# A chunked delta-rule recurrence on one core: states and deltas in two halves, another order of the calls, waits against constants

## What is computed

```python
def _step(Sm, inputs):
    q_t, k_t, v_t, beta_t = inputs
    Sk = jnp.einsum('bhde,bhe->bhd', Sm, k_t)
    delta = v_t - Sk
    Sm = Sm + beta_t[..., None] * jnp.einsum('bhd,bhe->bhde', delta, k_t)
    o_t = jnp.einsum('bhde,bhe->bhd', Sm, q_t)
    return (Sm, o_t)
_, outputs = jax.lax.scan(_step, S0, (q, k, v, beta))
return outputs @ wo + bo
```

## Time and profile before

| what | value |
|---|---|
| time, median of 3 runs (lowest to highest) | 3310.53 us (3310.06 to 3311.02) |
| profiled execution, first to last instruction | 3309.8 us |
| PE busy, weight loads busy | 3179.2 us (96%), 2594.1 us (78%) |
| DVE, ACT, POOL busy | 1841.6 us (56%), 1308.4 us (40%), 1205.1 us (36%) |
| recurrence, first and last small matmul of the stage | 962.7 and 1721.4 us |
| in it, first matmul of product 0 and of product 63 | 998.2 and 1717.9 us |

### The profile page before, as it was taken

One profiled execution on the slowest core, in us unless ns is written; L12 is line 12 of the kernel. 1 busy time (PEld: TensorE's weight loads), 2 busy tenths in 40 slices (PEclk: granted clock), 3 DMA queues, 4 the chain that ended last, 5 costly groups with the idle time before them and its releaser, 6 DMA issues.

```text
span 3309.8 us, 150288 instructions
## 1 busy us (share of the span) xinstructions
PE 3179.2 (96%) x68438; PEld 2594.1 (78%) x68438; DVE 1841.6 (56%) x2965; ACT 1308.4 (40%) x2654; POOL 1205.1 (36%) x1211
## 2 busy tenths in 40 slices
PE   5999999999958999999999999999999999999998
PEld 4777777777747888898888778887777888777886
DVE  6787878778648899888323333233333323333324
ACT  5444445444313333333343333333333433333333
POOL 1435564655526776666211222211222212122211
PEclk8999999999969999999999999999999999999999
DMA  3445555455465677666661110101110110111010
GB/s 111 144 148 167 141 162 154 145 152 162 139 201 181 220 227 228 215 197 207 200 184 35 39 39 13 39 26 39 39 39 17 36 39 26 39 39 38 14 39 26
DMA packets 388865, 356.00 MB, mean 108 GB/s; under 512 B 58256, under 2 KB 321680, under 8 KB 385680
## 3 DMA queue, kind: packets, MB, share of 16 engines
q1 hardware_dynamic: 386400, 351.86, 34.2%
q10 hardware_dynamic: 2224, 0.90, 0.2%
HBM read 184.65 MB, written 153.09 MB: 102 GB/s over the span
## 4 chain that ended last, share of the span: by engine, by line
PE 65%; DMA 2%; SPq 0%; DVE 0%; issue 0%; ACT 0%; DVEq 0%; ACTq 0%
PE bank L237 14%; PE bank L235 14%; PE bank L236 14%; PE bank L1238 13%; PE bank L1283 5%; PE bank L1698 2%; PE bank L1689 2%; DMA ringB<-heads_scratch 1%; PE bank L1681 1%; PE bank L1672 1%; DMA Z<-z_scratch 0%; DVE g L2010 0%; PE bank L1745 0%; SPq L1147 0%; ACT relu L1867 0%
## 5 line engine op out<-in xcount | busy, mean ns | idle before, releaser
L1939 DVE TENSOR_TENSOR glo<-gl,gh 128x512 fp32r<-128x512 f32 x256 | 196.0, 766 | 823.5 <-ACT gh L1817 821.8
L1813 ACT ACTIVATE gl<-bank,b1m 128x512 f32<-128x512 f32 x256 | 176.0, 687 | 736.4 <-PE bank L237 730.9
L235 PE MATMUL bank<-h,w_hi 128*128 128x512 f32 x1024 | 421.1, 411 | 0.1
L235 PE MATMUL bank<-w_hi,gh 128*128 128x512 f32 x1024 | 402.7, 393 | 0.9 <-DVE glo L1939 0.9
L237 PE MATMUL bank<-h,w_lo 128*128 128x512 f32 x1024 | 401.3, 392 | 0.0
L237 PE MATMUL bank<-w_hi,glo 128*128 128x512 f32 x1024 | 400.5, 391 | 0.0
L236 PE MATMUL bank<-h,w_hi 128*128 128x512 f32 x1024 | 399.4, 390 | 0.0
L236 PE MATMUL bank<-w_lo,gh 128*128 128x512 f32 x1024 | 399.2, 390 | 0.0
L236 PEld LDWEIGHTS bank<-h,w_hi 128*128 128x128 f32 x1024 | 193.4, 189 | 49.2 <-issue 10.7
L235 PEld LDWEIGHTS bank<-h,w_hi 128*128 128x128 f32 x1024 | 192.5, 188 | 48.7 <-issue 10.8
L1238 PE MATMUL bank<-ringA 32*32 32x32 f32 x16512 | 221.9, 196 | 5.3 <-issue 4.3
(11 more groups left out here) (200 smaller groups left out, 7086.1 us busy)
## 6 DMA issues: line engine op xcount, KB each, us to landing
ringB<-heads_scratch SPq DMA_DIRECT2D x257, 192.0 KB, 3.3
ringA<-heads_scratch SPq DMA_DIRECT2D x260, 128.0 KB, 2.8
X<-in_L_attn_x SPq DMA_DIRECT2D x16, 1024.0 KB, 10.1
x_scratch<-X SPq DMA_DIRECT2D x16, 1024.0 KB, 4.5
heads_scratch<-vb SPq DMA_DIRECT2D x16, 1024.0 KB, 5.2
heads_scratch<-qk SPq DMA_DIRECT2D x16, 1024.0 KB, 6.6
heads_scratch<-kb SPq DMA_DIRECT2D x16, 1024.0 KB, 5.2
heads_scratch<-kbuf SPq DMA_DIRECT2D x16, 1024.0 KB, 7.2
```

The costliest lines, as they stand in the source:

```text
L235: e.matmul(o, lhs[0], rhs[0], start=first, stop=False)
L1813: e.activation(gl[k][:, :], bank[1 - k][:, :], ACT.Gelu_apprx_tanh, bias=b1m[:, m:m + 1]).then_inc(a_gl, 1)
L1939: e.tensor_tensor(gh[k][1][:, :], gl[k][:, :], gh[k][0][:, :], ALU.subtract).then_inc(v_gl, 1)
```

## The change

The state, the delta and their copies are cut into two halves of two head groups each (FRONT and BACK), each with a bank of its own: `B_DELTA` is (4, 5) by half instead of by pair of chunks, `B_STATE` is (6, 3), and `B_R` is one bank instead of two. A call of `delta`, `state`, `values` or `out_delta` is then 8 matmuls; `keys` and `out_state` stay at 16. ACT makes four copies of 128x64 per chunk (two of the delta, two of the state) instead of two of 128x128, and one of R as before. The outputs of a chunk are computed within that chunk, `keys` and `values` of the next chunk too, and `out_product` stands in the block's chunk 1.

`a_delta` and `a_state` become four semaphores each, one per slot of the ring. PE waits for them, and for `d_A` and `d_B`, against constants, and three matmuls of each chunk take the counts back down (`then_inc(d_A[j], -32)` and so on). Three waits keep a register: `v_olo` twice and `v_z` once per block. SP loads in another order (`load_a` and `load_b` of one chunk side by side; `load_x1`, `store_z` and `load_system` at other places), `high` and `low` move by a chunk or two, and the low parts of w1 are made by POOL (`o_w1lo`) in chunk 3 of a block, no longer by DVE in chunk 2. POOL's memset fills the slot 3 of `ringB` at the start, so PE waits for fewer transfers before its loop.

```diff
-        B_WO, B_R, B_DELTA, B_STATE, B_OUT = 0, (1, 3), (4, 5), 6, (7, 2)
+        B_WO, B_R, B_DELTA, B_STATE, B_OUT = 0, 1, (4, 5), (6, 3), (7, 2)
+        FRONT, BACK = 0, 1
...
+            def chunk(j):
+
+                after, before = (j + 1) % 4, (j + 3) % 4
+                e.wait_ge(a_state[j], 1)
+                made = delta(j, FRONT)
+                made[0].then_inc(d_A[j], -32)
+                made[1].then_inc(a_delta[before], -2)
+                made[2].then_inc(d_B[before], -16)
+                e.wait_ge(d_A[after], 32)
+                keys(after)
+                e.wait_ge(a_state[j], 2)
+                delta(j, BACK)
+                e.wait_ge(d_B[j], 16)
...
+            def rest(j):
+
+                after = (j + 1) % 4
+                out_state(j)
+                e.wait_ge(a_delta[j], 1)
+                state(j, FRONT)
+                values(after, FRONT)
+                out_delta(j, FRONT)
+                e.wait_ge(a_delta[j], 2)
+                state(j, BACK)
+                values(after, BACK)
...
+                    chunk(0)
+                    e.wait_ge(v_olo, out)
+                    e.reg_add(out, out, 4)
+                    rest(0)
+                    outs_back(0)
+
+                    chunk(1)
+                    rest(1)
+                    e.wait_ge(v_olo, out)
+                    e.reg_add(out, out, 4)
+                    e.wait_ge(v_z, done)
+                    e.reg_add(done, done, 8)
+                    outs_back(1)
+                    out_product(range(12))
+
+                    for j in (2, 3):
+                        chunk(j)
+                        rest(j)
+                        outs_back(j)
...
             def delta(c):
-                e.wait_ge(p_delta, c + 1)
-                e.activation(heads(de[c % 2][:, :, :]), bank[B_DELTA[(c // 2) % 2]][:, c % 2 * P:(c % 2 + 1) * P],
-                             ACT.Copy).then_inc(a_delta, 2)
+                for h in range(2):
+                    e.wait_ge(p_delta, 2 * c + h + 1)
+                    e.activation(heads(de[c % 2][:, 2 * h:2 * h + 2, :]), bank[B_DELTA[h]][:, 0:P // 2],
+                                 ACT.Copy).then_inc(a_delta[c % 4], 1)
...
-                i = piece2(blk)
-                if at == 2 and i is not None:
-                    e.wait_ge(a_w1hi, i + 1)
-                    e.tensor_tensor(pieces2[i][2], w1s[i % 2], pieces2[i][1], ALU.subtract).then_inc(v_w1lo, 1)
...
+                i = piece2(blk)
+                if at == 3 and i is not None:
+                    e.wait_ge(a_w1hi, i + 1)
+                    e.tensor_tensor(pieces2[i][2], w1s[i % 2], pieces2[i][1], ALU.subtract).then_inc(o_w1lo, 1)
```

230 lines of the change are left out of this document (91 added, 139 removed).

## The result

| | median us (lowest to highest) | ratio to the kernel before, 95% interval |
|---|---|---|
| kernel before, same chip | 3310.8 (3310.1 to 3312.1) | |
| changed kernel | 3337.4 (3332.8 to 3339.6) | 1.0077 [1.0065, 1.009] |

The change costs 27 us where 34 were to be gained. The span of the profiled execution grew from 3309.8 to 3331.0 us; for the changed kernel the fastest of its four runs was profiled, so the trace shows 21 of the 27 us. Here are the stretches, cut as in the earlier trace rows (the columns are length, then busy time and records of PE, PEld, DVE, ACT and POOL, the granted clock, DMA share and GB/s): the start, a light block, a heavy block with the solver, a block without it, the two blocks around a `load_system` (the later one first), block 53 and the one behind it, and blocks 7 to 52.

A forecast was written before the change was run, and what follows sets the result against it. PE was taken as bound by register waits and hand-overs, both at 0.98 to 1.00 us. A block of 10.67 against 11.08 gave 23; 23 + 10 - 2.5 + 3 = 33.5 off 3309.8, forecast 3277, range 3250 to 3307.

The forecast's parts named there:

- constant waits: On first matmuls of 23 calls per block, waits against constants: 0.01 each, 0.2 per block (bounds 0 and 2.1).
- call ends: 36 calls per block instead of 24; each end costs up to 0.02 us, so 12 more add 0.24.
- free waits: Rival, chance 0.12: constant waits and call ends cost nothing, the block is 10.2 us, the kernel 3252.
- the loop's end, which no product covers any more, 0.15: End of PE's loop: one of three register-wait sites left per block, 0.15 us of their 0.45.
- PE may be almost two chunks ahead of it, which evens this out: In the loop, PE's lead over DVE evens out DVE's heaviest blocks, 10.91 us busy against 10.0 on average.
- DVE binds: Rival, chance 0.15: heavy blocks run at DVE's 10.9 us, only the 11 without a solver at 10.67; kernel 3288.
- Loads: 2.5 lost: System-load blocks: PE's wait for `ringA` is 1.5 us, 0.5 more than before, in 5 blocks (bounds 0 and 10).
- The start: 10: Products 0 to 5: DVE gets its first `low` some 10 us sooner, 10 us won (bounds 3 and 13).
- Block 53: SP is held there and 4.5 us are lost; a longer lead gives back about 3 (bounds 0 and 4).
- w1: Low parts moved from DVE to POOL: DVE saves 0.92 and loses 0.96 each, so nothing was counted.
- Both limits lie at 0.98 to 1.00: taking away one alone would leave the other: In PE's block, calls with register waits and whole hand-overs of delta and state were taken as equal limits.
- The rival that ended slower, 3351: Chance 0.10: 16 hand-overs per block instead of 8, each late by 0.08 us; block 11.97, 51 us lost, 10.5 won.

The follow-up runs named there:

- e6: Kernel before, with only its waits on copies and ring loads set against constants, on counters taken down again: 3302.5 us, 0.9977 of the kernel before.
- e3: Changed kernel with ACT's `high` of output 2b moved from behind chunk 2's state copies to the end of chunk 1: 3327.3 us, 1.0057.
- e7: Changed kernel with e1 and e3 together: 3317.8 us, 1.0017 of the kernel before.
- e1: Changed kernel with TensorE's loop turned so that its end follows the product, same order of matmuls: 3339.3 us, 1.0088.
- e12: e6 with system loads split in four, then low-part waits made constant and the wait ahead of the product dropped: 3309.3 us, against 3307.3 without the last two edits.
- e2: Changed kernel with every solver multiplication and addition cut to one column, so solved systems are not the reference's: 3328.0 us, 1.0053.
- e11: e7 with the system's 2 MB cut into four loads of 512 KB, one a block: 3319.7 us, 1.0027.
- e9: e7 with the later system load of e5: 3315.4 us, 1.0015.
- e4: Changed kernel with the low parts of w1 made by DVE in chunk 2 again instead of POOL: 3338.0 us, 1.0086.
- e8: e3 with both copies of a delta or state waiting for the second half call: 3386.0 us, 1.0221.
- e5: e3 with the system's load put behind the ring loads for chunk c + 7 instead of ahead of them: 3327.6 us, 1.0048.

## Why the prediction was wrong

The forecast block was 10.67 us. In the same parts as the table: product 2.96, calls 6.72 + 0.20 + 0.24 = 7.16, gaps 0.45 + 0.10 = 0.55. Measured without a solver: 2.95, 7.18 and 1.20; with it 2.95, 7.18 and 1.55.

- **What PE issues came out near, in part by luck.** A half call takes 0.14, the copy of 64 columns 0.22 to 0.23. The calls together are 7.18 against 7.16 (6.90 by the border of 33 ns). But two counts in that sum were too low: a chunk has 10 calls (8 half, 2 whole), so a block has 40 and not 36, and 16 more ends than before, 0.32 by my price and not 0.24; and PE posts 24 more counts per block, not 20 (in the trace 41 against 17 with the product's), since a fourth matmul of each chunk takes `a_state` down in `outs_back`, where I had named three. The shares are uncertain: constant waits and counts take 0.01 to 0.12 inside the calls, by the border (e6; I had 0.20), and the call ends with the rest of the new order 0.1 to 0.35 (e3 and e7 against e6). The rival *free waits* is out, since no form of the changed kernel has a block under 10.9 where it forecast 10.2; what a posted count costs by itself no run separates. By the Trainium skill's 26 ns per increment (TensorE: Matmul & The Clock Gate, "The cost: per-tile semaphore tail") the 24 more counts alone would be an estimated 0.62; the calls grew by 0.37 at most with everything in them, so here not all of that tail is seen in issue.
- **The step that failed first is "the loop's end, which no product covers any more, 0.15".** It is 0.505, and e1 takes all but 0.06 of it away. I priced a loop's back edge like a register wait. The bound I gave, 0.30, did not hold it either, and no row of before showed a back edge uncovered: there it stood behind the product's last matmul, where the 0.32 to the next one's start are the same with a back edge and without. That is 0.35 a block, 20 us over 57 blocks. I had also not seen that about 0.12 of before's gaps, ahead of the product, are no wait (e12) and stay, and left out small gaps of 0.04 to 0.06 where a constant wait stands. These two make up most of the other 0.3.
- **The second is "PE may be almost two chunks ahead of it, which evens this out".** That fits before, where in DVE's list both `low` of a block's outputs stand in chunks 0 and 1 of the next block and the product is due behind its chunk 3. Now the second `low` stands in chunk 0 and the product is due at the end of chunk 1, and the first `high` stands behind chunk 2's copies. The ring cost 8.4 us (e3). As the *DVE binds* rival put it, a block would have been DVE's busy 10.9; it was 12.1 at a busy time of 10.84, because idle time inside a ring counts.
- **"Loads: 2.5 lost"** had the stop right in three of five systems, 1.53 to 1.61 against 1.5, but not what follows it there: the clock at half for 3.4 us and the next block's delay. Five pairs of blocks take 126.6 us against 116.1, which is 10.5 lost, of which 3 are the growth that all blocks have; 8.5 of it lie in the three pairs with the lower clock. Why the clock fell in these three stays open. In before the stops of up to 1.25 in these blocks had no fall behind them, but the length of the stop alone does not decide it: after stops of 1.72, 2.13 and 2.16 in e2, of 1.70 in e3 and of 1.97 in e11 it stayed at 1.00, and with one of 1.41 in e9 it fell.
- **"The start: 10"** was counted by a mark that the change moves. Product 5 comes 9.3 us sooner and product 6 9.1, but 4.0 of these 9.1 only say that the product stands two chunks earlier in the program; the sum took them as won and left out the two chunks that now stand behind product 63. By the same chunk the start wins 5.1: 4.1 of them are there at the loop's first `delta`, and only 1.0 comes from DVE's first `low` and all else up to block 6.
- **Block 53 was right, w1 in the total**: 2.8 against 3 in blocks 53 and 54; nothing for w1, though by two differences that cancel (e4). POOL's `w_lo` did hold DVE up: beside it the addition of 128x660 took 1.65, where the larger 128x684 took 1.16 beside one of POOL's solver operations. That is what the Trainium skill (SBUF — State Buffer, "Who interferes with whom") says of such a pair.
- **"Both limits lie at 0.98 to 1.00: taking away one alone would leave the other"** is half right. The register waits lay 0.2 us a block higher; e6 takes them and is 8.7 us faster. The change's other half was a loss of 0.10 to 0.14 in the blocks with a solver even where nothing hides it (e7 against e6), and a gain of 0.07 in those without. I had read those blocks as 11.0 in before; they are 11.19 on average, and in one of them the trace names the `de` copy for waits of 0.23 and 0.10, so there the hand-over was the longer limit.

The rival that ended slower, 3351, came close in time but not in cause: no copy is late by its own length, and e8, where they are late, takes 1.2 us a block more. Against the kernel before the 21 us of the two spans are: 0.3 a block in blocks 7 to 52, 14 us (by the table, 0.4 more calls and 0.5 of loop's end, against some 0.6 of waits saved); the ring's part in blocks without a load, 6; the blocks around the system loads, 7 beyond that; 1.5 in blocks 55 to 63; and, counted by the same chunk, about 1 behind the last block, against 8 won at start and in blocks 53 and 54.

## What to carry to other kernels

When a program is reordered, look at what the work stood over before: here a loop's back edge cost nothing under long matmuls and half a microsecond between short ones, so end the loop behind its longest instruction. An engine's idle time is only spare if it lies outside the ring of hand-overs: follow one whole turn from product to product through every engine's list, in the new order, before calling an engine free. Count what is won by a mark that the change does not move, such as the first call of a chunk. Where two limits seem equal, make the cheap edit of the pair alone first: here the constant waits by themselves, some 30 lines, beat both kernels, and the rest of the change, even repaired (e7), stayed behind them.

## What the runs showed of the hardware

- A back edge of TensorE's loop takes 0.505 us from one small matmul to the next (0.06 at the same place without it, e1). Behind the matmuls of 128x512 it costs nothing that shows: 0.32 to the next small one with it (before, e1) and without it (changed kernel).
- A wait against a register takes some 0.14 us from one small matmul to the next, one against a constant 0.04 to 0.05 (0.10 at three places in front of `state` and `delta` in e6); in front of a change from 32x32 to 128x512 matmuls the register wait costs nothing beyond the 0.12 of the change itself (e12).
- Around stops of 1.53 to 1.61 us for a load, the granted clock fell to 0.50 for 3.4 us in three system blocks of the changed kernel; in those of e6, whose stops are of up to 1.14 us, it stayed at 1.00. In e2 it also stayed there after stops of 1.72 to 2.16 us, so a stop of that length does not always bring it down.
- Turning the loop, which needs a second copy of its code, made product 6 come 3.2 us later and the way from product 63 to the third stage 6.9 us longer (e7 against e3), 4.4 of it with PE idle and no releaser shown. That is 10 us of the some 24 that it gives back at 0.42 a block.
- The load of 2 MB delayed what was issued after it in both places where it was put (changed kernel, e5, e9), and four loads of 512 KB held the DMA engines busy for more time (share 0.83 against 0.71 at 218 and 219 GB/s), not less.
